# One 512-column product for the high weights of the second half

## The reference

```python
scores = jnp.where(mask, jnp.einsum('bld,d->bl', x, aw), -jnp.inf)
feature = jnp.einsum('bl,bld->bd', softmax(scores), x)
g_h = relu(jnp.einsum('bd,hdk->bhk', feature, gW1) + gb1)
gate = softmax(jnp.einsum('bhk,hke->bhe', g_h, gW2) + gb2, axis=-1)[arange(b), D]
h1 = relu((jnp.einsum('bd,edk->ebk', feature, eW1) + eb1) * inv1 + bn1_b)
h2 = relu((jnp.einsum('ebk,eko->ebo', h1, eW2) + eb2) * inv2 + bn2_b)
rep = jnp.einsum('be,ebo->bo', gate, h2)
out = softmax((jnp.einsum('bo,hoc->bhc', rep, hW) + hb)[arange(b), D])
```

## Time and profile before

| | us |
|---|---|
| median of 3 runs | 606.93 (606.55 to 607.15) |
| profiled execution, its own time | 607.16 |
| its span in the profile | 605.4 |
| outside of the span | 1.8 |
| TensorE busy | 516.6 (85%), 4191 products |
| TensorE weight loads | 415.8 (69%) |
| VectorE busy | 483.5 (80%) |
| ScalarE busy | 454.7 (75%) |
| GpSimd busy | 81.1 (13%) |

### The profile page before, as it was taken

The page is one execution under the profiler, slowest core; times in us unless marked ns, Lnnn a source line. Parts: engine busy times, 40 slices in busy tenths (PEclk is TensorE's granted clock), DMA queues, the critical chain, the costliest instruction groups (busy, mean ns, idle before and its releaser), DMA issues.

```text
span 605.4 us, 11281 instructions
## 1 busy us (share of the span) xinstructions
PE 516.6 (85%) x4191; PEld 415.8 (69%) x4191; DVE 483.5 (80%) x961; ACT 454.7 (75%) x1007; POOL 81.1 (13%) x118
## 2 busy tenths in 40 slices
PE   0376564875699999999999989999999999999994
PEld 0111121211688888778878778889999999999994
DVE  6989999996899989879999997565376666657663
ACT  5989999997699899879998985455545665665651
POOL 0000000000110220201111111111211222222200
PEclk9967888767699999999999999999999999999998
DMA  8999999999999999999999744455555665666510
GB/s 315 401 363 401 401 401 401 379 405 404 402 388 375 355 387 386 348 370 326 329 370 356 272 132 125 153 168 163 180 158 156 178 183 190 170 188 191 167 69 0
DMA packets 52338, 168.05 MB, mean 278 GB/s; under 512 B 4796, under 2 KB 5040, under 8 KB 52284
## 3 DMA queue, kind: packets, MB, share of 16 engines
q1 hardware_dynamic: 36012, 100.88, 43.9%
q0 software_dynamic: 16128, 66.07, 33.6%
q10 hardware_dynamic: 144, 0.39, 0.2%
HBM read 167.32 MB, written 0.00 MB: 276 GB/s over the span
## 4 chain that ended last, share of the span: by engine, by line
PE 53%; DMA 24%; DVE 13%; issue 5%; ACT 5%; SPq 0%; ACTq 0%; DVEq 0%
DMA xring<-in_r_x_dram 24%; PE z_ps L852 14%; PE z_ps L853 14%; PE z_ps L854 14%; DVE prod_out L617 6%; DVE wlo L605 4%; PE feat_ps L914 4%; PE z_ps L883 4%; ACT copy_out L421 2%; ACT whi L406 2%; DVE h_hi L673 1%; DVE h L693 1%; PE turn_ps L947 0%; PE turn_ps L960 0%; DVE h_lo L675 0%
## 5 line engine op out<-in xcount | busy, mean ns | idle before, releaser
L617 DVE CUSTOM_DVE_ANT_0 prod_out<-xring,aw_bc 128x768 bf16<-128x768 f32 x256 | 233.3, 947 | 11.0 <-DMA xring<-in_r_x_dram 10.4
L421 ACT ACTIVATE copy_out<-xring 128x768 bf16<-128x768 f32 x256 | 212.7, 832 | 13.5 <-DMA xring<-in_r_x_dram 12.6
L852 PE MATMUL z_ps<-feat_hi,whi 128*128 128x256 f32 x720 | 207.4, 288 | 1.5 <-DVE feat_lo L652 1.2
L605 DVE TENSOR_TENSOR wlo<-wraw,whi 128x1152 fp32r<-128x1152 f32 x106 | 143.4, 1354 | 77.4 <-ACT whi L406 76.1
L853 PE MATMUL z_ps<-feat_lo,whi 128*128 128x256 f32 x720 | 204.7, 284 | 0.0
L854 PE MATMUL z_ps<-feat_hi,wlo 128*128 128x256 f32 x720 | 204.6, 284 | 0.0
L406 ACT ACTIVATE whi<-wraw 128x1152 fp32r<-128x1152 f32 x106 | 122.7, 1158 | 61.3 <-PE z_ps L854 61.3
L852 PEld LDWEIGHTS z_ps<-feat_hi,whi 128*128 128x128 f32 x720 | 139.1, 193 | 3.2 <-DVE feat_lo L652 1.6
L853 PEld LDWEIGHTS z_ps<-feat_lo,whi 128*128 128x128 f32 x720 | 139.2, 193 | 0.0
L854 PEld LDWEIGHTS z_ps<-feat_hi,wlo 128*128 128x128 f32 x720 | 139.0, 193 | 0.0
L914 PE MATMUL feat_ps<-xring,pwin 128*32 128x384 f32 x1024 | 116.8, 595 | 20.4 <-ACT pwin L439 20.3
(11 more groups left out here) (97 smaller groups left out, 331.6 us busy)
## 6 DMA issues: line engine op xcount, KB each, us to landing
xring<-in_r_x_dram SPq DMA_DIRECT2D x128, 768.0 KB, 8.1
wraw<-in_L_rec_eW_dram POOLq DMA_DIRECT2D x90, 576.0 KB, 4.5
wraw<-in_L_rec_gW_dram POOLq DMA_DIRECT2D x16, 576.0 KB, 5.8
w2raw<-in_L_rec_eW_dram POOLq DMA_DIRECT2D x6, 576.0 KB, 5.6
aw_bc<-in_L_rec_aw_dram ACTq DMA_DIRECT2D x1, 384.0 KB, 5.6
w2raw<-in_L_rec_gW_dram SPq DMA_DIRECT2D x1, 48.0 KB
h<-in_L_rec_eb_dram SPq DMA_DIRECT2D x1, 24.0 KB
h<-in_L_rec_bn_g_dram SPq DMA_DIRECT2D x1, 24.0 KB
```

What stands on the lines that cost most here:

```text
L421: nc.scalar.activation(copy_out[:, t % 2, :], xring[:, r % RING_ROUNDS, j, i, :], ACT.Copy, accum_out=rowsum[:, r % 2, t:t + 1]).then_inc( ...
L605: nc.vector.tensor_tensor(wlo[:, split_slot(u), :, :], wraw[:, raw_slot(u), :, :], whi[:, split_slot(u), :, :].bitcast(F32), ALU.subtract) ...
L617: nc.vector.tensor_tensor_reduce(out=prod_out[:, t % 2, :], in0=xring[:, r % RING_ROUNDS, j, i, :], in1=aw_bc[:, :], scale=1.0, scalar=0.0 ...
L852: nc.tensor.matmul(psum_tile, w_hi, a_hi, start=first, stop=False)
```

## The change

In the second half every unit that is not a gate ("wide") makes two products where it made three: the high weight tile meets high and low activations side by side in one product of 512 columns, into the whole bank, and the low weight tile meets the high activations in the first 256 columns. For that, the high and low parts lie next to each other in feat and in h1s. The bank's right half then holds high weight x low activation. ScalarE reads that half with scale and bias (Identity, no relu) and counts part_ready; VectorE then adds the left half times scale in `join_parts`, and it is now VectorE that counts z_read. The relu moves to the next use: a max in the two instructions of split_h1 and in the gate product of add_expert. The joins of tiles 0 and 1 stand at the end of VectorE's slot, that of tile 2 ahead of the low part in the next slot.

```diff
+        def is_wide(u):
+            c, kind, _, _ = UNITS[u]
+            return c == NCH - 1 and kind != "g"
...
-        feat_hi = sb("feat_hi", [P, NCH, KT, CHUNK], F32R)
-        feat_lo = sb("feat_lo", [P, NCH, KT, CHUNK], F32R)
+        feat = sb("feat", [P, NCH, KT, 2, CHUNK], F32R)
+        feat_hi, feat_lo = feat[:, :, :, 0, :], feat[:, :, :, 1, :]
...
-        h1_hi = sb("h1_hi", [P, KT, CHUNK], F32R)
-        h1_lo = sb("h1_lo", [P, KT, CHUNK], F32R)
+        h1s = sb("h1s", [P, KT, 2, CHUNK], F32R)
+        h1_hi, h1_lo = h1s[:, :, 0, :], h1s[:, :, 1, :]
...
             def read_tile(panel, m, dest, col, scaled):
                 act.wait_ge(z_ready, tiles(panel, m))
                 src = z_ps[:, (MT * panel + m) % ZB, 0:CHUNK]
+                if is_wide(2 * panel):
+                    nc.scalar.activation(dest, z_ps[:, (MT * panel + m) % ZB, CHUNK:2 * CHUNK], ACT.Identity,
+                                         bias=bias[:, col:col + 1], scale=scale[:, col:col + 1]).then_inc(part_ready, 1)
+                    return
...
+            def join_parts(u, ms):
+                c, kind, q, half = UNITS[u]
+                if half == 0 or not is_wide(u):
+                    return
+                panel = u // 2
+                for m in ms:
+                    if kind == "c":
+                        dest, col = h2[:, m, :], N1 + HT * q + m
+                    else:
+                        t = MT * "ab".index(kind) + m
+                        dest, col = h1[:, t, :], KT * q + t
+                    dve.wait_ge(part_ready, wide_tiles(panel, m))
+                    nc.vector.scalar_tensor_tensor(out=dest, in0=z_ps[:, (MT * panel + m) % ZB, 0:CHUNK],
+                                                   scalar=scale[:, col:col + 1], in1=dest, op0=ALU.mult,
+                                                   op1=ALU.add).then_inc(z_read, 1)
...
                 ks = slice(KU * half, KU * half + KU)
+                if c == NCH - 1:
+                    nc.vector.tensor_scalar(h1_hi[:, ks, :], h1[:, ks, :], 0.0, None, ALU.max).then_inc(h1_hi_ready, 1)
+                    dve.wait_ge(h1_hi_ready, h1_count(c, q, half))
+                    nc.vector.scalar_tensor_tensor(out=h1_lo[:, ks, :], in0=h1[:, ks, :], scalar=0.0,
+                                                   in1=h1_hi[:, ks, :].bitcast(F32), op0=ALU.max,
+                                                   op1=ALU.subtract).then_inc(h1_ready, 1)
+                    return
...
+                if c == NCH - 1:
+                    nc.vector.scalar_tensor_tensor(out=h2[:, :, :], in0=h2[:, :, :], scalar=0.0, in1=gates, op0=ALU.max,
+                                                   op1=ALU.mult).then_inc(gated_ready, 1)
...
+                if s:
+                    join_parts(s - 1, (2,))
                 split_lo(s + AHEAD)
                 for c, q, half in H1_SLOT.get(s, ()):
                     split_h1(c, q, half)
...
                     add_expert(*ADD_SLOT[s])
+                join_parts(s, (0, 1))
+            join_parts(SLOTS - 1, (2,))
...
+            def wide_products(z, w_hi, w_lo, a, first, last):
+                if not first:
+                    nc.tensor.matmul(z[:, 0:CHUNK], w_lo, a[:, 0, :], start=False, stop=False)
+                ins = nc.tensor.matmul(z, w_hi, a.rearrange("p a n -> p (a n)"), start=first, stop=last)
+                if first:
+                    ins = nc.tensor.matmul(z[:, 0:CHUNK], w_lo, a[:, 0, :], start=False, stop=False)
+                return ins
```

More of the change, by code:

```diff
@@ L103, in split_slot, with wide_tiles @@
             return (SPLITS[u] - 1) % SPLIT
+        def is_wide(u):
+            c, kind, _, _ = UNITS[u]
+            return c == NCH - 1 and kind != "g"
+        def wide_tiles(panel, m):
+            return MT * sum(is_wide(2 * p) for p in range(panel)) + m + 1
         def tiles(panel, m):
@@ L270, in rec_kernel @@
         z_read = sem("z_read")
+        part_ready = sem("part_ready")
         h1_hi_ready = sem("h1_hi_ready")
@@ L692, in add_expert @@
                 dve.wait_ge(z_read, tiles(panel_of(c, "c", q), MT - 1))
-                nc.vector.tensor_tensor(h2[:, :, :], h2[:, :, :],
-                                        gate_bc.unsqueeze(1).to_broadcast([P, HT, CHUNK]),
-                                        ALU.mult).then_inc(gated_ready, 1)
+                gates = gate_bc.unsqueeze(1).to_broadcast([P, HT, CHUNK])
+                if c == NCH - 1:
+                    nc.vector.scalar_tensor_tensor(out=h2[:, :, :], in0=h2[:, :, :], scalar=0.0, in1=gates, op0=ALU.max,
+                                                   op1=ALU.mult).then_inc(gated_ready, 1)
+                else:
+                    nc.vector.tensor_tensor(h2[:, :, :], h2[:, :, :], gates, ALU.mult).then_inc(gated_ready, 1)
                 dve.wait_ge(gated_ready, n + 1)
@@ L862, in unit @@
                         pe.wait_ge(h1_ready, h1_count(c, q, half))
-                        a_hi, a_lo = h1_hi, h1_lo
+                        a_hi, a_lo, a = h1_hi, h1_lo, h1s
                     else:
-                        a_hi, a_lo = feat_hi[:, c, :, :], feat_lo[:, c, :, :]
+                        a_hi, a_lo, a = feat_hi[:, c, :, :], feat_lo[:, c, :, :], feat[:, c, :, :, :]
                     slot = split_slot(u)
@@ L876, in unit @@
                         kk = KU * half + k
-                        if is_split(u):
+                        if is_wide(u):
+                            last = wide_products(z_ps[:, (MT * panel + m) % ZB, :], whi[:, slot, k, cols],
+                                                 wlo[:, slot, k, cols], a[:, kk, :, :], kk == 0, kk == KT - 1)
+                        elif is_split(u):
                             last = products(z, whi[:, slot, k, cols], wlo[:, slot, k, cols], a_hi[:, kk, :],
```

## The result

The changed kernel takes 626.79 us (median of 4 runs, 623.70 to 627.51), the kernel before 607.04 (606.55 to 607.62): ratio 1.0311, 95% interval 1.028 to 1.0341. It is 3% slower. I had forecast 620.2 with a range of 609 to 626: the sign was right, the size 6.6 us too small, the median 0.8 above the range (the ratio on the 606.93 that the forecast started from gives 625.8, just inside).

What follows compares the result with a forecast made beforehand. VectorE was taken to bound the first half and TensorE the second. Terms 0.85 (head), 9.1 (second-half stalls net of saved products), 0.44 (tail) and 2.9 (first-half casts) gave +13.3 us: 620.2, range 609 to 626.

Steps and rivals of the forecast that it cites:

- Part 1, the products: Second half's wide units: 512-column product at 0.216, triple 0.36 to pair 0.336, saving 10.4 us of TensorE's work.
- Part 2, the cast: VectorE's high cast of h1 loses its double rate writing three runs with gaps: 0.55 to 0.96 us, +0.41.
- Part 2, the join: VectorE's join, reading 256 PSUM elements: 0.41 us to its end, 0.33 to the next start.
- Part 3, the walk: Second half, slot by slot: TensorE stalls for late tile joins; 20.87 us per expert against 19.55, +9.1 from first to last.
- b1: Last of an expert's six units; add_expert delays its joins, then TensorE stalls 1.50 us, seven times, 10.5 in all.
- a1: Second of an expert's six units; the h1 split delays its joins, then TensorE stalls 1.11 us, six times, 6.7 in all.
- U: Start of an odd unit (half 1); TensorE was to want tile 1 of the next panel at U + 4.03.
- First half: Six h1 casts in VectorE's chain and one at 403.09, each 0.41 longer: +2.9 us.
- Rival 1: VectorE's h1 cast keeps 0.55; expert period 20.08, +3.9 us in all, 611; chance 0.27.
- Rival 2: The 512-column product takes 0.227 to 0.24: 623 at 0.227, about 627 at 0.24 with slow casts; chance beyond 0.23 0.08.
- Rival 3: TensorE doesn't wait for tile 1 joins, 597; chance 0.06, shared with any other faster outcome.
- Rival 4: Wide units bound by VectorE's total work, no saving; put at 16.3 of 20.9 us per expert, not deciding; no separate chance.

Runs made afterwards that it cites:

- half-column: Kernel before, with the high-weight, low-activation product in the second half's experts cut to 128 of 256 columns: 604.47 us in one run.
- wide-alone: Changed kernel with early joins, wide units leaving out the low-weight products so that 512-column products follow each other: 595.81 us in one run.
- plain layout: Changed kernel with h1's high parts in one block and low parts in another, so the cast writes one run of 768: 617.6 us, ratio 1.0168.
- gaps-alone: Kernel before, with only h1_hi and h1_lo laid into one h1s as three runs of 256 with gaps: 611.74 us, ratio 1.0077.
- TensorE kept busy: Ten extra unread products ahead of each of two TensorE waits: on the changed kernel 624.1 us; on the kernel before with h1's gaps 610.93 us.
- placed kernel: Changed kernel with h1's parts in two blocks, joins early except last in the gate's slot and behind the h1 split in head_pick's: 606.24 us, ratio 0.9983.

## Why the prediction was right or wrong

**Part 1, the products: mis-sized.** I took 0.216 for the wide product from the fp32 row and read the twelve products of 8 columns as "the weight load sets the pace, not the columns". That reading was wrong: the 1.57 of that row runs up to the release of VectorE, its parts start 0.112 to 0.114 apart, so the load alone doesn't make 0.12; and the columns of fp32r cost nearly as much (the half-column and the wide-alone runs). Nor are the rows what I took them for: L883 issues nine fp32 products in a unit and the trace has 18 rows for them (108 for 54 in all), so 0.216 is half of one fp32 product, and no measure of a fp32r product of 512 columns. A wide product costs 0.233 in the pairs and 0.227 alone, between my bounds of 0.216 and 0.24 and nearer the upper. An expert's products take 19.00 us, not 18.26: 0.55 saved, not 1.29, and 8 x 0.55 = 4.4 us in all for my 10.4. This is the step that put the time above the forecast: six periods came out 0.43 to 0.45 longer each, 2.7 us where 3.2 were missing in all; 1.2 more came ahead of and behind them and 0.8 in the last products, less the 1.3 of luck in the x phase and 0.2 in the first half.

**Part 2, the cast: right.** 946 and 937 ns for the 0.96 taken; +0.39 for +0.41. No row of before showed it; the plain layout's 554 and 544 do. By the Trainium skill's rule (VectorE: DVE Perf Modes, Mode 2×_2P — use both read ports for one tensor) this had to be so, and the trace agrees in both layouts.

**Part 2, the join: near.** 0.48 long and 0.39 to the next start, for 0.41 and 0.33; TensorE is released 0.53 after its start, for 0.41 + 0.14.

**Part 3, the walk: right in place, 0.3 too long.** Fourteen waits, seven behind b1, six behind a1, one at the head's slot, none behind c1, as walked. They lose 1.30 and 1.00 us an expert for 1.50 and 1.11. This error follows from that of part 1 and takes back some of it: a unit is 3.15, not 3.02, so tile 1 is wanted at U + 4.20, not U + 4.03, 0.17 later at both places: 2.61 - 0.34 = 2.27, measured 2.30.

**First half: right.** 2.7 us up to the gate logits for seven casts at 2.9; the six on VectorE's chain are 2.35 in the gaps-alone run, for 2.5.

**Not in the sum: the clock.** I priced each stall at its own length. But where TensorE idles for about two us and more, at 404 to 406, at the gate and at the end, the clock falls in some executions: of the traces kept, four have it below 0.7 from 408 to 411, that of the change has 1.00. It is 0.8 us in the tail of the profiled execution, and most likely the 2.7 us between the median of the change and that of the change with TensorE kept busy. That puts the median 0.8 above my range, which the profiled execution is within.

**The rivals.** Rival 1 (the cast keeps its rate) fell with its row; what it would have given, 611, was 617.6 when tried, for the most part since it too rested on 0.216: its period came out at 20.73, not 20.08. Rival 2 was the case that came: the pair costs 0.350, between the 0.347 and the 0.36 of its two figures, 623 and 627, and the profiled 623.7 fits the first. I gave it 0.08 beyond 0.23, for a reading of one row. Rival 3 (no waits, 597) needed joins out of the way, and with them out of the way it is 606.24: 6 of the 9 us are the same 0.216 (4.4 saved, not 10.4). Rival 4 fell: VectorE at 45 of 50 us holds up nobody.

## What to carry to other kernels

When one instruction replaces two, find out first which of load and columns sets the old pace; where the two are nearly equal, taking away a load saves next to nothing, and a row with another data type can't stand in for the missing one. Read a pace from starts inside a stream: a row that begins behind a wait, or a chain's piece that ends at a release, is longer than its products. An instruction put at the end of an engine's slot inherits the worst slot's queue: price the deadline of what it releases, put it right behind the work it needs in the slots in which others follow, and behind a chain that is itself waited for. A new layout is paid in each instruction that writes it, also where the change is not used.

## What the runs showed of the hardware that I had not expected

- At full clock and with a weight load each, fp32r products of 512 columns start 0.227 us apart, those of 256 columns 0.12; in pairs the wide one costs 0.233 and the narrow one 0.117. A fp32 product is two rows in the trace, with a load each, 0.216 apart at 256 columns (L883) and 0.112 at 8 (L960). A product cut from 256 to 128 columns among full ones gives back 0.01. The Trainium skill (TensorE: Matmul & The Clock Gate, Back-to-back issue gap) gives N / 2.4 + 2.5 ns for the gap of an isolated product, by which 512 columns would take 215.8 ns; in the streams here it is 227 to 233, and the measurement decides.
- TensorE's granted clock fell to 1.2 GHz after idle time of 1.82 us (gaps alone), with products 0.21 apart; in the change it idled for the same 1.82 us (restart at 406.24) and the clock stayed at 1.00. The twelve last products took 2.36 us in the change and 1.50 in the one without gaps, each after 3.15 us of idling, and 1.55 after 2.62 in the kernel before. It falls in some executions of one kernel and not in others: the gaps-alone runs spread over 2.8 us, and over 0.5 with TensorE kept busy.
- Without gaps the high part of h1 takes 0.55 us in one slot and 0.71 in another (524.66 and 515.60 in the placed kernel). The longer one starts 0.4 us after GpSimd began a load's issue of 0.76 us (515.19); the other has none beside it at its start (the next begins at 525.04, within its last 0.2 us). That the two are cause and effect was not tried.
